# Row factors and power of a retention layer on GpSimd, later tiles normalised on ScalarE

## The reference, cut to what matters

```python
q = x @ q_w + q_b
k = (x @ k_w + k_b) * SCALING
v = x @ v_w + v_b
g = x @ g_w + g_b
...
qk = jnp.einsum('bhmd,bhnd->bhmn', qr, kr) * mask
denom = jnp.clip(jnp.abs(jax.lax.stop_gradient(qk).sum(axis=-1, keepdims=True)), 1.0, None)
qk = qk / denom
out = jnp.einsum('bhmn,bhnd->bhmd', qk, vr).transpose(0, 2, 1, 3)
mu = out.mean(axis=-1, keepdims=True)
var = out.var(axis=-1, keepdims=True)
out = (out - mu) / jnp.sqrt(var + 1e-05)
out = out.reshape(bsz, slen, N_HEADS * HEAD_DIM)
out = jax.nn.silu(g) * out
return out @ o_w + o_b
```

## Time and profile before

| | value |
|---|---|
| median of 3 runs (lowest, highest) | 1046.27 us (1046.23, 1047.78) |
| the profiled execution, its own time | 1045.22 us |
| its span, first to last instruction | 1043.5 us |
| busy: PE, PE weight loads, DVE | 913.1 us (88%), 565.3 us (54%), 754.9 us (72%) |
| busy: ACT, POOL | 601.3 us (58%), 350.1 us (34%) |
| mean granted TensorE clock | 0.957 |
| HBM over the span | 20 GB/s |

### The profile page before, as it was taken

One profiled execution on the slowest core, in us unless ns is written; L12 is line 12 of the kernel. 1 busy time (PEld: TensorE's weight loads), 2 busy tenths in 40 slices (PEclk: granted clock), 3 DMA queues, 4 the chain that ended last, 5 costly groups with the idle time before them and its releaser, 6 DMA issues. The chain is left out here.

```text
span 1043.5 us, 20376 instructions
## 1 busy us (share of the span) xinstructions
PE 913.1 (88%) x8028; PEld 565.3 (54%) x8028; DVE 754.9 (72%) x1412; ACT 601.3 (58%) x1052; POOL 350.1 (34%) x310
## 2 busy tenths in 40 slices
PE   2778878899589799999689999998799988999996
PEld 1323333333247545565456777776699974455554
DVE  8957978895778899887768899886678865344412
ACT  4778969999567553552145555554688853332410
POOL 1314764563237231000246667675243210000000
PEclk9969989999779999999999999999899999999999
DMA  5000000000221030000130000000200000000001
GB/s 145 0 2 1 1 2 1 1 1 1 67 96 42 1 133 1 1 2 1 46 120 2 2 1 2 3 2 1 72 2 1 3 1 1 1 13 9 21 1 41
DMA packets 17502, 21.96 MB, mean 21 GB/s; under 512 B 4656, under 2 KB 14590, under 8 KB 17024
## 3 DMA queue, kind: packets, MB, share of 16 engines
q1 hardware_dynamic: 15296, 18.57, 5.5%
q10 hardware_dynamic: 2112, 2.10, 0.6%
HBM read 18.56 MB, written 2.10 MB: 20 GB/s over the span
## 5 line engine op out<-in xcount | busy, mean ns | idle before, releaser
L625 PE MATMUL t_sc<-t_qk 32*128 32x512 f32 (+3 forms) x768 | 117.2, 571 | 41.4 <-ACT t_pT L515 16.2
L515 ACT ACTIVATE t_pT<-t_sc 128x1536 f32<-128x1536 f32 x96 | 136.7, 1453 | 23.8 <-PE t_sc L625 22.9
L3081 DVE SCALAR_TENSOR_TENSOR f_h<-f_psh,f_h 128x512 f16<-128x512 f32 x64 | 43.9, 691 | 100.8 <-ACT f_h L3107 100.7
L3137 PE MATMUL f_psh<-f_h,fs_w 128*128 128x512 f16 x512 | 114.4, 379 | 1.5 <-DVE f_h L3081 1.5
L229 POOL TENSOR_SCALAR_AFFINE_SELECT t_pT<-t_pT 128x512 f32<-128x512 f32 x64 | 75.1, 1196 | 112.7 <-ACT t_pT L515 112.4
L625 PEld LDWEIGHTS t_sc<-t_qk 32*128 32x128 f32 x768 | 53.2, 203 | 104.9 <-ACT t_pT L515 61.3
L3107 ACT ACTIVATE f_h<-f_psh 128x512 f16<-128x512 f32 x64 | 38.2, 597 | 108.4 <-PE f_psh L3137 108.4
L2600 POOL TENSOR_SCALAR_AFFINE_SELECT r_att<-r_att 128x1024 f16<-128x1024 f16 x64 | 69.6, 1110 | 66.2 <-DVE r_att L2640 66.0
L645 PE MATMUL t_ot<-t_pT,t_v 128*17 128x512 f32 (+3 forms) x768 | 73.6, 511 | 9.4 <-issue 8.8
L3137 PEld LDWEIGHTS f_psh<-f_h,fs_w 128*128 128x128 f16 x512 | 49.8, 98 | 59.0 <-issue 2.0
L1896 PE MATMUL c_pso<-ck_VO,c_pT 128*128 128x256 f16 x480 | 55.0, 273 | 1.4 <-DVE c_pT L1747 1.4
(11 more groups left out here) (504 smaller groups left out, 2175.2 us busy)
## 6 DMA issues: line engine op xcount, KB each, us to landing
x<-in_x ACTq DMA_DIRECT2D x4, 512.0 KB, 7.6
out_x<-x SPq DMA_DIRECT2D x4, 512.0 KB, 2.9
r_rcos<-in_ret_cos SPq DMA_DIRECT2D x1, 1280.0 KB, 8.0
r_rsin<-in_ret_sin SPq DMA_DIRECT2D x1, 1280.0 KB, 10.5
gw_raw<-in_gateT SPq DMA_DIRECT2D x1, 1024.0 KB, 7.1
gw_raw<-in_upT SPq DMA_DIRECT2D x1, 1024.0 KB, 9.1
gw_raw<-in_downT SPq DMA_DIRECT2D x1, 1024.0 KB, 4.7
fs_k<-in_L_ffn_k SPq DMA_DIRECT2D x1, 1024.0 KB, 7.4
```

Of the source, the lines that this page charges most:

```text
L515: a.activation(pT[:, at:at + 3, :].rearrange("p a s -> p (a s)"), sc[n % 2][:], ACT.Exp, scale=CURVE * CURVE / math.sqrt(2 * DH)).then_inc ...
L625: last = t.matmul(sc[n % 2][:, 512 * k + at:512 * k + at + w], qk[r, g % 2, 1, P * i:P * i + P], qk[r, g % 2, 0, q0:q0 + w], start=(part = ...
L3081: v.scalar_tensor_tensor(dst[:, 1], psh[:, i % BANKS, :], 0.0, dst[:, 0], ALU.max, ALU.subtract).then_inc(lo_done, 1)
L3137: last = mm(psh[:, i % BANKS, :], l, r, start=(k == 0), stop=(k == len(todo) - 1))
```

## The change

Three things, all in the retention and in `Ahead`:

- The row factors go from DVE to POOL. The floor table now has two parts per head, one over the root of the row total and VD times EPS times the total. POOL's `power(t)` multiplies the weight sum by the first, squares it, takes the maximum with 1, multiplies by the second, adds the sum of the squares, and then takes the power: five small operations on 128 x 16 ahead of the power, each waiting for the one before it. DVE's `centre(t)` keeps only the sum of the squares. The division by VD is gone from the variance, and the root of VD goes into the output's scale and the bias instead.
- Tiles 4 to 15 are normalised by ACT (one activation with Identity, scale and bias per row) at the end of step s, behind silu, instead of by DVE near the start of it.
- For that, DVE forms minus mean times inverse root twice (`offsets`), in steps -2 and 1, each time as the first thing behind `low(s, 0)`.

```diff
-    floor = lay(EPS * total)
+    floor = lay(np.concatenate([1.0 / np.sqrt(total), VD * EPS * total], 1))
...
+    def offsets(self, v, n):
+
+        t = slice(*self.SPANS[n])
+        v.wait_ge(self.rs_ready, n + 1)
+        v.scalar_tensor_tensor(self.sm[:, 0, t], self.sm[:, 1, t], -1.0, self.sm[:, 3, t], ALU.mult, ALU.mult).then_inc(self.nm_ready, 1)
+
+    def center_on_scalar(self, a, t):
+
+        a.wait_ge(self.nm_ready, sum(t >= b for b, _ in self.SPANS[1:]))
+        wait(a, self.turned, t - 1)
+        a.activation(self.xn[:, t % 2, 0:D - 1], self.x[:, t, 0:D - 1], ACT.Identity, bias=self.sm[:, 0, t:t + 1],
+                     scale=self.sm[:, 3, t:t + 1]).then_inc(self.normed, 1)
...
-        rfloor, keep = sb("rfloor", [P, TB, HR]), sb("keep", [P, 4])
+        rfloor, keep = sb("rfloor", [P, TB, 2, HR]), sb("keep", [P, 4])
...
             def power(t):
                 if inside(t):
                     q = t % 2
-                    g.wait_ge(centred, t + 1)
-                    g.tensor_tensor(sm[:, q, 2, :], sm[:, q, 1, :], ahead.sm[:, 4, 0:1].broadcast_to((P, HR)), ALU.pow).then_inc(pow_done, 1)
+                    low_, var = sm[:, q, 0, :], sm[:, q, 1, :]
+                    g.wait_ge(s_norm, 2 * 16)
+                    g.wait_ge(cen_done, t + 1)
+                    own.link(g.tensor_tensor(low_, cen[:, q, :, VD], rfloor[:, t % TB, 0, :], ALU.mult))
+                    own.link(g.tensor_tensor(low_, low_, low_, ALU.mult))
+                    own.link(g.tensor_scalar(low_, low_, 1.0, None, ALU.max))
+                    own.link(g.tensor_tensor(low_, low_, rfloor[:, t % TB, 1, :], ALU.mult))
+                    g.wait_ge(sq_used, t + 1)
+                    own.link(g.tensor_tensor(var, var, low_, ALU.add))
+                    g.tensor_tensor(sm[:, q, 2, :], var, ahead.sm[:, 4, 0:1].broadcast_to((P, HR)), ALU.pow).then_inc(pow_done, 1)
...
             def centre(t):
...
-                    low_, var = sm[:, q, 0, :], sm[:, q, 1, :]
-                    v.wait_ge(s_norm, 2 * 16)
-                    v.wait_ge(cen_done, t + 1)
-                    L(v.scalar_tensor_tensor(low_, cen[:, q, :, VD], EPS, cen[:, q, :, VD], ALU.mult, ALU.mult))
-                    L(v.tensor_tensor(low_, low_, rfloor[:, t % TB, :], ALU.max))
+                    wait(v, pow_done, t - 1)
                     v.wait_ge(sq_done, t + 1)
-                    v.tensor_reduce(var, sq[:], AX_X, ALU.add).then_inc(sq_used, 1)
-                    v.wait_ge(sq_used, t + 1)
-                    v.scalar_tensor_tensor(var, var, 1.0 / VD, low_, ALU.mult, ALU.add).then_inc(centred, 1)
+                    v.tensor_reduce(sm[:, q, 1, :], sq[:], AX_X, ALU.add).then_inc(sq_used, 1)
...
             for s in STEPS:
                 low(s, 0)
-                x_center(s + 5)
+                if s == STEPS[0]:
+                    ahead.offsets(v, 1)
+                if s == STEPS[0] + 3:
+                    ahead.offsets(v, 2)
                 gate(s - 2)
...
                 silu(s - 1)
+                x_center(s + 5)
```

More of the change, by code:

```diff
@@ L2330, in __init__ @@
         self.made, self.var_ready, self.rs_ready = sem("made"), sem("var_ready"), sem("rs_ready")
-        self.normed, self.turned = sem("normed"), sem("turned")
+        self.normed, self.turned, self.nm_ready = sem("normed"), sem("turned"), sem("nm_ready")
         self.high_done, self.ready = sem("high_done"), sem("ready")
@@ L2468, in on_vector @@
             v.wait_ge(self.b_high, 2)
-            v.scalar_tensor_tensor(self.b16[r, 0:D], self.brow[r], GAIN, self.bhi[r, 0:D], ALU.mult, ALU.subtract).then_inc(self.b_ready, 1)
+            v.scalar_tensor_tensor(self.b16[r, 0:D], self.brow[r], GAIN / math.sqrt(VD), self.bhi[r, 0:D], ALU.mult, ALU.subtract).then_inc(self.b_ready, 1)
         if event == (2, 3):
@@ L2508, in on_scalar @@
             r = slice(self.LO_ROW, self.LO_ROW + 1)
-            a.mul(self.bhi[r, 0:D], self.brow[r], GAIN).then_inc(self.b_high, 1)
-            a.mul(self.b16[0:1, 0:D], self.brow[0:1], GAIN).then_inc(self.b_high, 1)
+            a.mul(self.bhi[r, 0:D], self.brow[r], GAIN / math.sqrt(VD)).then_inc(self.b_high, 1)
+            a.mul(self.b16[0:1, 0:D], self.brow[0:1], GAIN / math.sqrt(VD)).then_inc(self.b_high, 1)
         if event == (1, 6):
@@ L2555, in retention @@
         names = ("qk_ready rot_done q_turned q_copied k_turned k_copied v_psum v_done "
-                 "g_psum silu_done scored hi_done lo_done kept_state masked vhi_done vlo_done d_ready u_done pv_done cen_done sq_done sq_used centred pow_done "
+                 "g_psum silu_done scored hi_done lo_done kept_state masked vhi_done vlo_done d_ready u_done pv_done cen_done sq_done sq_used pow_done "
                  "z_ready z_turned zhi_done z_split o_ready x_added").split()
         (qk_ready, rot_done, q_turned, q_copied, k_turned, k_copied, v_psum, v_done,
-         g_psum, silu_done, scored, hi_done, lo_done, kept_state, masked, vhi_done, vlo_done, d_ready, u_done, pv_done, cen_done, sq_done, sq_used, centred, pow_done,
+         g_psum, silu_done, scored, hi_done, lo_done, kept_state, masked, vhi_done, vlo_done, d_ready, u_done, pv_done, cen_done, sq_done, sq_used, pow_done,
          z_ready, z_turned, zhi_done, z_split, o_ready, x_added) = [sem(n) for n in names]
@@ L2575, in _ @@
         def _(sp):
-            for dst, nm in ((rfloor, "floor"), (keep, "keep")):
-                sp.dma_start(dst[:], ins["ret_" + nm]).then_inc(s_norm, 16)
+            for dst, nm in ((rfloor[:].rearrange("p t a h -> p t (a h)"), "floor"), (keep[:], "keep")):
+                sp.dma_start(dst, ins["ret_" + nm]).then_inc(s_norm, 16)
             for some, done in ((slice(1, 3), s_next), (slice(3, TB), s_tab), (slice(0, 1), s_tab)):
@@ L2652, in x_low @@
                     ahead.low(v, t, psq)
-            def x_center(t):
-                if inside(t) and t >= FIRST:
-                    ahead.center(v, t)
             def gate(t):
@@ L2716, in add @@
                     v.wait_ge(o_ready, t + 1)
-                    v.scalar_tensor_tensor(x[:, t, :], psd[:, 256:512], 1.0 / GAIN, x[:, t, :], ALU.mult, ALU.add).then_inc(x_added, 1)
+                    v.scalar_tensor_tensor(x[:, t, :], psd[:, 256:512], math.sqrt(VD) / GAIN, x[:, t, :], ALU.mult, ALU.add).then_inc(x_added, 1)
             def z_low(t):
@@ L2797, in x_high, with x_center @@
                     ahead.high(a, t, psq)
+            def x_center(t):
+                if inside(t) and t >= FIRST:
+                    ahead.center_on_scalar(a, t)
             for s in STEPS:
```

## The result

| | before | after |
|---|---|---|
| median of 22 runs each, on the same chips (lowest, highest) | 1048.71 us (1045.25, 1054.31) | 1051.4 us (1048.47, 1056.51) |
| ratio, 95% interval | | 1.003 [1.0018, 1.0042] |
| the profiled execution, its own time and span | 1045.22, 1043.5 | 1055.88, 1054.1 |
| busy: DVE, ACT, POOL | 754.9, 601.3, 350.1 | 727.8, 607.5, 370.6 |
| mean granted TensorE clock | 0.957 | 0.951 |

The change makes the kernel slower by 1.9 to 4.4 us, 3.1 in the middle. The work moved as intended: DVE is busy for 27 us less, POOL for 20 us more and ACT for 6 us more. None of what DVE gave up came back as time.

The account below looks back on a forecast made before the run. PE was taken to bound the retention's middle, so only its ends count: 0.20 + 0.48 + 1.2 = 1.9 us, nothing against it. From a median of 1046.27 this gave 1048.2 us, range 1045.6 to 1050.0.

Parts of the forecast that it names:

- PE sets the pace in the middle, what DVE gives up is worth nothing: Middle steps: PE waits for nobody, so DVE's freed time shortens nothing; steps stay 12.43 us apart.
- The five operations, 0.21 us each and 0.30 apart: POOL ahead of the power: five small operations of 0.21 us, 0.30 us apiece with waits, 1.5 us in all.
- The dear POOL operation: Rival, slower: 0.50 us apiece on POOL from a 0.38 us fixed part, sum 2.9 us, 1049.2 us; chance 0.22.
- The signs named in advance: Profile after: 12.43 us steps, DVE idle near 3 us before scores, POOL operations 0.21 us, tile 14's gate awaiting power.
- The product with `keep`: On DVE in the middle: the state's product would take up part of the 1.06 us spent behind POOL's mask.
- The sign of being wrong: Would refute the forecast: a middle step not 12.43 us, or a last gate that did not wait for POOL.
- The start, 0.20 + 0.48: Pipeline start: DVE's offsets ahead of the first rotation 0.20 us, tile 4's normalisation before scores' copy on ACT 0.48 us.
- The power of tile 14 comes 1.2 us later: Pipeline end: POOL's power 1.3 us later, less 0.1 us slack, delays PE's transposes and what follows by 1.2 us.
- POOL has 4.0 us of gaps, steps grow only over 0.83 us per operation: Middle steps: POOL's idle time before the two masks, 1.34 and 2.66 us, holds five operations up to 0.83 us apiece.
- The gate's second operation has 1.5 us of slack: Middle steps: POOL's power ends 1.9 us before DVE's gate needs it, 1.5 us with the gate 0.4 us earlier.
- The clock: Rival, slower: a low TensorE clock stretch lasts 3 us longer, half is lost, 1.5 us, 1049.7 us; chance 0.10.
- The time of 1048.2 and "about the same": Whole kernel: median 1048.2 us, 1.9 us over 1046.27; a change within 0.2% was given 0.52.

Follow-up runs that it names:

- e1: The kernel before with only ACT's normalisations and DVE's offsets, row factors staying on DVE; retention 208.97 us against 208.40 before.
- e7: e6 with the statistics and spread of tiles 12 to 15 behind the first rotation; 1048.82 us in 10 runs, ratio 1.0017 to before.
- e6: The changed kernel with four small POOL operations between the masks, tile 4 normalised on DVE, offsets behind the rotation; 1047.56 us, ratio 1.0002 to before.
- e10: The changed kernel with POOL's maximum done seven times and DVE's gate behind the rotation; steps 12.72 us, retention 221.24 us.
- e3: The changed kernel with tile 4 normalised on DVE again and the offsets behind the rotation; retention 210.33 us against 210.68.
- e4: The changed kernel with POOL's power for the next stage in step 13 instead of 14; retention 210.41 us against 210.68.
- e9: The changed kernel with POOL's maximum done four times, three more operations per tile; steps 12.43 us, retention 212.66 us.
- e8: The changed kernel with POOL's maximum done seven times, six more operations per tile; steps 13.15 us, retention 226.84 us.
- e5: The changed kernel with four of the five small POOL operations moved between the two masks; retention 209.11 us against 210.68.

## Where the prediction was right and where wrong

- **PE sets the pace in the middle, what DVE gives up is worth nothing:** right. Steps are 12.43 us apart in before, the changed kernel and e1 to e7, and e6 with 27 us less DVE work takes the time of before. The rule of the Trainium skill on reading a trace (Trainium Kernel Development and Optimization, Performance Expectations, Reading a trace), by which matmul busy time is a bad measure of how close a kernel is to its limit and weight loads are a good one, would have favoured a gain; here the matmul rows were the bound, with the weight loads at 9.02 of 12.43 us.
- **The five operations, 0.21 us each and 0.30 apart:** right, 0.22 to 0.25 and 0.30 to 0.33. The dear POOL operation is refuted. The estimate of 0.095 us from the figures of the Trainium skill (GPSIMD Engine Reference, sections 3.1 and 4.1) is too low for operations this small.
- **The signs named in advance:** the steps and the new operations came as said. DVE's idle time before the scores did not: 1.29 us as before instead of nearly 3, since what DVE gained now goes into a wait for PE (614.93). The product with `keep` didn't take up the 1.06 us either: it begins at 615.26, 0.01 behind the mask's end, and takes 0.34. In e10, where it starts under a mask, it takes 1.16 to 1.17 us in eight of sixteen cases. The sign of being wrong, a last gate that did not wait for POOL, came true by its words, for the gate of tile 15 had its power 0.8 us ahead; the same text had said that of this gate, and the one that must wait is that of tile 14, which did.
- **The start, 0.20 + 0.48:** oversized. 0.08 + 0.37, together 0.45 instead of 0.68; with 0.05 from the clock the trace has 0.50. ACT started the copy 0.50 us behind the normalisation, but the normalisation only 0.47 behind the values' second copy, which the scores' copy had followed at 0.60. The rotation doesn't depend on the offsets and started before they had ended, so an inserted operation cost its issue interval of 0.08 us and not the 0.20 of a linked chain. e3 shows that nothing else in the ACT part costs within the retention.
- **The power of tile 14 comes 1.2 us later:** undersized. This is the step of the sum that failed. The transposes of tile 14 come 1.73 us later than the start accounts for (2.23 less 0.50). 1.38 of them are the five operations and their power, close to the forecast: 1.59 us from the first operation to the power where I had 1.5, 0.14 off for the early start (I had 0.17), 0.10 off for slack as I had it, and a power 0.03 longer. The other 0.35 had no term at all: I let the delay of one power act on its own gate, and did not follow POOL's queue past the power of tile 13 to the masks of tile 15. There the five operations act a second time, and the power of 13, grown by 0.5 us, and the foreign power of step 14 fill the queue. e4 takes 0.31 of the 0.35 us back, e9 shows the double count.
- **The retention 1.9 us longer:** 2.28 to the last transposes (0.50, 1.73 and 0.05 behind it), 2.09 to the next stage. The mechanism was right, the size 0.2 to 0.4 us short.
- **Nothing behind the retention:** the sum has no term there, and the traces have 0.9 to 1.0 us in the next stage. Up to the end of the program the change costs 2.8 to 2.9 us instead of 1.9. Why, no run settles.
- **POOL has 4.0 us of gaps, steps grow only over 0.83 us per operation:** wrong, though nothing in the forecast hung on it. The gaps before the masks are POOL's part of a loop with DVE. The real slack was 1.15 us, and e8 passed it with six operations. Had the five been dear, 0.53 us apiece would have been enough (1.15 / 5 over the 0.30).
- **The gate's second operation has 1.5 us of slack:** it had 1.04 (power's end at 607.74, gate at 608.78); the 0.5 us are the power's growth.
- **The clock:** no extra low spell in the retention of the changed kernel, so this rival didn't come true there. In e7 it did, for another edit, and e9 has a further low spell from 721.5 to 724.9 us, which costs its marks nothing: PE still idles 0.59 us before the transposes of tile 14. In the next stage the spells come later than before, as told above.
- **The time of 1048.2 and "about the same": wrong.** The result, 1051.4, lies 1.4 us above the range, and slower by over 0.2% is what happened. The larger failed step is the base of the sum: the median of three runs, 1046.27, lies at the low end of what 22 runs of the same kernel give (1048.71), 2.4 of the 3.2 us between forecast and result. The range held the terms of the change and no uncertainty of the base. From the base of 22 runs the same terms give 1050.6. The other 0.8 us are the cost itself, 2.7 us between the two medians where the sum had 1.9: the undersized term at the end of the retention and the missing one behind it.
- **The side of the 0.2% line:** the forecast stood 0.2 us under the line of 2.1 us. The retention alone, with 2.28 us, crosses it, and the time has 3.1 [1.9, 4.4].

## What to carry to other kernels

Moving work off an engine that waits for the bound gains nothing; ask first who waits for nobody, and then price only the pipeline's two ends. In hand-ordered queues, spare time on an engine is not the sum of its idle gaps: follow the loop of waits through the other engines once round, and compare its length with the step. Small linked operations belong into a gap that their inputs already allow (e5 won back 1.57 of 2.28 us by order alone), not in front of what others wait for.

## What the hardware did that I had not expected

**POOL's power took 3.41 us instead of 2.90 when DVE had started a certain operation just before it.** The 0.5 us show exactly when DVE's remainder of the values, which reads two SBUF tiles, starts a few hundredths earlier. From e2, the kernel with the POOL part alone, in two successive steps:

```profile
572.83 0.68 DVE L2669 TENSOR_TENSOR r_v<-r_v 128x512 f16<-128x512 f32 x1
572.88 3.41 POOL L2640 TENSOR_TENSOR r_sm<-r_sm,ra_sm 128x16 f32<-128x16 f32 x1
...
585.27 0.71 DVE L2669 TENSOR_TENSOR r_v<-r_v 128x512 f16<-128x512 f32 x1
...
586.14 2.92 POOL L2640 TENSOR_TENSOR r_sm<-r_sm,ra_sm 128x16 f32<-128x16 f32 x1
```

Before, POOL had started first. The whole series, over thirteen traces (in e8 no power comes within 3 us of that operation), by how much POOL's power starts behind DVE's remainder:

| POOL behind DVE, us | power, us |
|---|---|
| POOL first, by 0.36 or more | 2.89 to 2.93 |
| 0.04 to 0.06 | 3.40 to 3.43 |
| 0.11, 0.12 | 3.35, 3.34 |
| 0.15 | 3.33 |
| 0.23, 0.27 | 3.25, 3.26 |
| 0.84 to 1.14 | 2.92 to 3.03 |
| 1.46 or more | 2.92 to 2.94 |

So the power is held up by part of what DVE's operation of 0.68 us still has to run, 0.5 us at the most. e8's first factor did the same: 0.69 us instead of 0.23, at 605.78 behind DVE's 605.71. The Trainium skill (SBUF — State Buffer, SBUF: two separate sides) has a rule for it: a DVE operation with two SBUF inputs and a GpSimd operation that reads SBUF exclude each other, and whichever starts first holds the access for its whole instruction. The trace agrees where DVE comes first. It doesn't where the power comes first: before, the power ran from 607.05 to 609.95, and DVE's remainder of the values (L2648), started at 608.38 in the middle of it, took 0.68 us as ever. Under a mask DVE does stand: L2677's 1.06 us.

In the middle steps the collision cost nothing; it only took 0.5 us of the loop's slack. At the end it did cost: the power of tile 13 is one of the long ones, and its 0.5 us are more than the 0.35 us by which the masks of tile 15 came late. No run took away the collision alone.

**The table attention takes 277.1 to 283.2 us in 14 traces of kernels that don't differ in it.** In the windows above the granted clock differs with it, 1.00 against 0.90; no run isolates the clock. The spread is more than the effect of this change, and the time of a single run can't judge it.
